# A four-layer graph network: all work between its edge stages laid out as pipelines over chunks of node blocks

## The reference, cut to what is computed

```python
# layer 0: attention (GATv2), 2 heads, with its own layer norm and relu ahead
h = relu(layernorm(x) * gamma + beta)
xl, xr = h @ Wl + bl, h @ Wr + br                      # [3125, 2*128]
alpha = softmax_by_dst((leaky_relu(xl[src] + xr[dst]) * att).sum(-1))
out = segment_sum(xl[src] * alpha, dst).mean(heads) + h @ res_W + bias + x
x = layernorm(x + out)
# layer 1: attention, 1 head, a scalar edge weight; gelu; batch norm over the nodes
m = leaky_relu((x @ Wl + bl)[src] + (x @ Wr + br)[dst] + edge_weight @ We)
h = gelu(x + segment_sum(alpha * xl[src], dst) + bias_out)
x = layernorm(x + (h - h.mean(0)) * rsqrt(h.var(0) + 1e-5) * bn_gamma + bn_beta)
# layer 2: three GINE layers
for l in range(3):
    agg = segment_sum(relu(y[src] + edge_attr @ W_lin[l] + b_lin[l]), dst)
    y = relu(batchnorm(relu((y + agg) @ W1[l] + b1[l]) @ W2[l] + b2[l]))
x = layernorm(x + y)
# layer 3: an MLP on every edge, its sum by target, an MLP on every node
e = relu(relu([x[src], x[dst], edge_attr] @ W1 + b1) @ W2 + b2) @ W3 + b3
node = relu([x, segment_sum(e, dst)] @ Wn1 + bn1) @ Wn2 + bn2
x = layernorm(x + layernorm(x + node) * gamma + beta)
```

## Time and profile before

| what | value |
|---|---|
| median of three runs | 4907.62 us |
| the profiled execution | 4908.47 us, span 4906.63, mean granted TensorE clock 0.802 |
| PE busy | 4209.5 us, 86% |
| PE's weight loads (PEld) | 3195.1, 65% |
| DVE | 2583.4, 53% |
| ACT | 1656.7, 34% |
| POOL | 2588.5, 53% |

### The profile page before, as it was taken

One profiled execution on the slowest core, in us unless ns is written; L12 is line 12 of the kernel. 1 busy time (PEld: TensorE's weight loads), 2 busy tenths in 40 slices (PEclk: granted clock), 3 DMA queues, 4 the chain that ended last, 5 costly groups with the idle time before them and its releaser, 6 DMA issues. The chain is left out here.

```text
span 4906.6 us, 91167 instructions
## 1 busy us (share of the span) xinstructions
PE 4209.5 (86%) x20501; PEld 3195.1 (65%) x20715; DVE 2583.4 (53%) x5638; ACT 1656.7 (34%) x3154; POOL 2588.5 (53%) x2647
## 2 busy tenths in 40 slices
PE   2799999947777649998799959999489999999994
PEld 1577777734444448886688848888356666666663
DVE  4788888866666544443344423444454555455544
ACT  1466666635555421112111121111233333333332
POOL 0455555437777537774577727777043434343420
PEclk9899999979999955555555555555799999999997
DMA  2333333323333212221222212222032222222210
GB/s 66 86 100 99 99 101 98 83 51 77 77 78 77 55 46 68 68 68 42 67 69 68 68 40 68 68 68 68 19 88 73 74 73 74 73 74 73 74 51 13
DMA packets 249457, 341.32 MB, mean 70 GB/s; under 512 B 102167, under 2 KB 174692, under 8 KB 249150
## 3 DMA queue, kind: packets, MB, share of 16 engines
q0 software_dynamic: 101632, 237.91, 18.2%
q1 hardware_dynamic: 130206, 78.84, 6.6%
q10 hardware_dynamic: 17568, 24.01, 1.7%
HBM read 324.54 MB, written 15.96 MB: 69 GB/s over the span
## 5 line engine op out<-in xcount | busy, mean ns | idle before, releaser
L771 POOL DMA_INDIRECT gath<-source_rows_narrow,idx x1176 | 1140.5, 970 | 613.9 <-issue 335.6
L894 POOL DMA_INDIRECT gath<-source_rows,idx_all x488 | 492.5, 1009 | 811.6 <-PE psum L913 561.2
L789 PE MATMUL psum<-gine_lin,ea 32*128 32x128 f32 x2928 | 757.3, 436 | 63.9 <-DMA ea<-in_edge_attr 63.4
L799 PE MATMUL psum<-hot,pm 128*128 128x128 f32 x2928 | 759.7, 441 | 36.7 <-ACT pm L854 36.2
L789 PEld LDWEIGHTS psum<-gine_lin,ea 32*128 32x128 f32 x2928 | 650.4, 323 | 148.2 <-DMA ea<-in_edge_attr 85.8
L799 PEld LDWEIGHTS psum<-hot,pm 128*128 128x128 f32 x2928 | 652.0, 328 | 121.8 <-issue 70.5
L552 POOL DMA_INDIRECT gath<-source_rows,idx_all x488 | 463.2, 949 | 482.7 <-PE psum L599 224.1
L854 ACT ACTIVATE pm<-vs 128x512 f32<-128x512 f32 x366 | 230.4, 629 | 1333.4 <-DVE vs L824 1313.5
L552 POOL DMA_INDIRECT gath<-source_rows_narrow,idx_all x488 | 487.0, 998 | 235.8 <-issue 148.1
L824 DVE TENSOR_TENSOR vs<-psum,gath 128x512 f32<-128x512 f32 x366 | 253.2, 692 | 635.1 <-POOLq L766 446.7
L582 PE MATMUL psum<-lk,att_b 128*128 128x512 f32 x732 | 373.4, 616 | 93.9 <-DVE lk L672 93.2
(11 more groups left out here) (188 smaller groups left out, 5609.9 us busy)
## 6 DMA issues: line engine op xcount, KB each, us to landing
rel<-rel_rows SPq DMA_DIRECT2D x366, 128.0 KB
ea<-in_edge_attr ACTq DMA_DIRECT2D x366, 64.0 KB
gath<-source_rows_narrow,idx POOLq DMA_INDIRECT x1176
gath<-source_rows,idx_all POOLq DMA_INDIRECT x976
gath<-source_rows_narrow,idx_all POOLq DMA_INDIRECT x488
ea<-in_edge_attr SPq DMA_DIRECT2D x122, 64.0 KB
source_rows<-stage SPq DMA_DIRECT2D x12, 512.0 KB, 2.9
source_rows_narrow<-TMP SPq DMA_DIRECT2D x3, 1600.0 KB, 7.3
```

Of the source, the lines that this page charges most:

```text
L771: pool.indirect_dma_start(out=gath[:, slot, j, 0:D], out_offset=None, in_=table1, in_offset=bass.IndirectOffsetOnAxis(ap=idx[:, slot, j:j ...
L789: last = e.matmul(E[s][:, j * D:(j + 1) * D], ea[:, s, j * P:(j + 1) * P], gine_lin[:, :], start=True, stop=True)
L799: last = e.matmul(O[s], pm[:, s, j * P:(j + 1) * P], hot[:, s, j, :], start=(j == 0), stop=(j == SUBS - 1))
L894: pool.indirect_dma_start(out=gath[:, i % 4, j, :], out_offset=None, in_=table, in_offset=bass.IndirectOffsetOnAxis(ap=idx_all[:, i, j:j + ...
```

## The change

Each stretch between two edge stages becomes one pipeline, or two, over seven chunks of four node blocks (`CB` = 4; the last chunk has one block). Each engine's instructions are written chunk by chunk, with semaphores that count chunks, so that no barrier stands between a norm, a turn and a product.

- **Row stages** (`rows_to_tables`, four calls): per chunk DVE computes mean and variance by `bn_stats` and `bn_aggr`, ACT the root, DVE reciprocal and shift, ACT the normalized rows (one instruction a block), PE turns them, ACT copies them (with gamma, beta and relu in layer 0), PE multiplies by Wl, DVE adds the bias, SP stores the chunk. On DVE the scale of a chunk comes behind the statistics of the next, and the bias add three chunks behind.
- **Target rows** (`TargetRows`) are not made in the row stage any more but at the head of the next edge stage, ahead of the walk on PE, ACT and DVE, while POOL's first gathers run. For the attentions their bias is a second matmul into the same bank: a row of ones (one partition) by the bias row. The first attention's also makes `Y` = 2x + h @ res_W + bias there. DVE's `memset` of `ACC` and its first `hot_t` come behind.
- **Setup** is merged into the first row stage: the loads are spread over SP's and ACT's queues, x comes in seven pieces, GINE's weights are all loaded here, the cutting of indices and edge weights is POOL's work instead of DVE's. The nine `weight_rows` stores are issued by SP at the end of the first attention's items.
- **Second row stage**: the heads' mean is one DVE instruction per block and head, inside the chunk.
- **End of the second attention** (`third_rows`): 25 sums, per chunk turned, gelu (with bias_out inside), statistics of 512 columns by `bn_stats`; then the batch norm's scale, and a second pipeline that shifts, turns back, adds the residual and makes GINE's first table with its bias.
- **GINE** is a Python loop over three layers. `gine_nodes`: seven adds, an MLP in chunks of 512 columns with two banks each way, `bn_stats`, then normalize, turn, add the bias and store by chunks; the last layer adds the residual instead.
- **Tail** (`node_out`): one pipeline of eight lags for the node MLP, both layer norms and the output, in rounds.

The core of the diff, with the new functions' loops:

```diff
-setup()
...
-with nc.Fori(0, GINE_LAYERS) as layer:
-    gine_node_to_table(layer)
-    gine_edges(layer)
-    gine_mlp(layer)
-    batchnorm("gine_bn", XT[:, :], gine_cols[:, 2:3], gine_cols[:, 3:4], ACT.Relu, sems=bn_sems, layer=layer)
-    transposes(XT, Z, *back_sems, base=layer * (NODE_BLOCKS // CH))
...
-node_mlp()
-transposes(HT, flat(Y))
-layernorm(Y[:, :, :], Y[:, :, :], gamma=bias("L3_gnn_gamma"), beta=bias("L3_gnn_beta"), prep=add_residual, prep_steps=1)
-layernorm(Y[:, :, :], Y[:, :, :], prep=add_residual, prep_steps=1)
...
+            for c in range(CHUNKS):
+                sp.wait_ge(row_staged, first_unit[c] + units_of[c])
+                sp.dma_start(out_rows[:, c * CB:c * CB + BLOCKS_OF[c], :],
+                             stage[:, c * CB:c * CB + BLOCKS_OF[c], :]).then_inc(row_stored, 16)
...
+            def stats(c):
+                a, n = c * CB, BLOCKS_OF[c]
+                if chunk_in is not None:
+                    v.wait_ge(chunk_in[c], 16)
+                if chunk_prep is not None:
+                    chunk_prep(v, step, a, n)
+                for b in range(a, a + n):
+                    last = v.bn_stats(row_stats[:, b, :], rows[:, b, :])
+                step(last)
+                for b in range(a, a + n):
+                    last = v.bn_aggr(row_mv[:, b, :], row_stats[:, b, :])
+                last.then_inc(row_var, 1)
+            def scales(c):
+                a, n = c * CB, BLOCKS_OF[c]
+                v.wait_ge(row_sd, base + c + 1)
+                step(v.reciprocal(row_scale[:, a:a + n], row_scale[:, a:a + n]))
+                v.scalar_tensor_tensor(row_shift[:, a:a + n], row_mv[:, a:a + n, 0], -1.0, row_scale[:, a:a + n],
+                                       ALU.mult, ALU.mult).then_inc(row_counted, 1)
...
+                for k in range(units_of[c]):
+                    u, m = first_unit[c] + k, min(per, n - k * per)
+                    v.wait_ge(row_made, u - unmade + 1)
+                    v.tensor_tensor(stage[:, a + k * per:a + k * per + m, :],
+                                    bank(u)[:, 0:m * width].rearrange("p (b w) -> p b w", w=width),
+                                    b_src.unsqueeze(1).broadcast_to([P, m, width]), ALU.add).then_inc(row_staged, 1)
...
+            if dve_first is not None:
+                dve_first(v, step)
+            for c in range(CHUNKS):
+                stats(c)
+                if c >= 1:
+                    scales(c - 1)
+                if c == 3 and bias_in is not None:
+                    v.wait_ge(bias_in, 16)
+                if c >= 3:
+                    add_bias(c - 3)
+            scales(CHUNKS - 1)
+            add_bias(CHUNKS - 3)
+            if dve_last is not None:
+                dve_last(v, step)
+            add_bias(CHUNKS - 2)
+            add_bias(CHUNKS - 1)
...
+            if act_first is not None:
+                act_first(a)
+            for c in range(CHUNKS):
+                deviations(c)
+                if c >= 1:
+                    normalize(c - 1)
+                if c == 2 and cols_in is not None:
+                    a.wait_ge(cols_in, 16)
+                if c >= 2:
+                    copy_turned(c - 2)
+            normalize(CHUNKS - 1)
+            copy_turned(CHUNKS - 2)
...
+            for c in range(CHUNKS):
+                turn(c)
+                if c == 1 and weights_in is not None:
+                    e.wait_ge(weights_in, 16)
+                if c >= 1:
+                    products(c - 1)
+            products(CHUNKS - 1)
+            if pe_last is not None:
+                pe_last(e)
...
+    def tensor(self, e):
+        w = self.width
+        for u in range(self.units):
+            a, m = self.blocks(u)
+            if u >= 4:
+                e.wait_ge(xr_rest, self.base + u - 3)
+            for j in range(m):
+                o = psum[:, u % 4, j * w:(j + 1) * w]
+                last = e.matmul(o, XT[:, (a + j) * P:(a + j + 1) * P], self.w_dst, start=True, stop=self.b_dst is None)
+                if self.b_dst is not None:
+                    last = e.matmul(o, ones_row[:, :], self.b_dst[0:1, :], start=False, stop=True)
+            last.then_inc(xr_made, 1)
+        if self.extra is not None:
+            for c in range(CHUNKS):
+                if c >= 4:
+                    e.wait_ge(xr_extra_out, c - 3)
+                for k in range(BLOCKS_OF[c]):
+                    o = psum[:, 4 + c % 4, k * D:(k + 1) * D]
+                    e.matmul(o, XT[:, (c * CB + k) * P:(c * CB + k + 1) * P], self.extra[0], start=True, stop=False)
+                    last = e.matmul(o, ones_row[:, :], self.extra[1][0:1, :], start=False, stop=True)
+                last.then_inc(xr_extra, 1)
+            e.wait_ge(xr_extra_out, CHUNKS)
+        e.wait_ge(xr_rest, self.base + self.units)
+        e.wait_ge(xr_third, self.base + self.units)
...
+        for u in range(self.units):
+            v.wait_ge(xr_first, self.base + u + 1)
+            if u >= 2:
+                v.wait_ge(xr_third, self.base + u - 1)
+            v.tensor_tensor(self.rest(u), self.bank(u), self.part(u, 0), ALU.subtract).then_inc(xr_rest, 1)
+            if u >= 1:
+                v.wait_ge(xr_rest, self.base + u)
+                third(u - 1)
...
+        step(pool.tensor_copy(dst_f, dst_i))
+        step(pool.tensor_scalar(dst_f, dst_f, gb_f[:, 2:3], -1.0, ALU.subtract, ALU.max))
+        step(pool.tensor_scalar(dst_f, dst_f, float(P), None, ALU.min))
+        pool.tensor_copy(src_f, src_i)
+        step(pool.tensor_copy(rel_b, dst_f))
+        pool.dma_start(rel_rows, rel_b).then_inc(rel_stored, 16)
+        pool.wait_ge(loads, 8 * 16)
+        m = [0]
+        for x, parts in ((ew_i, weight_parts), (we_f, we_p)):
+            for k, part in enumerate(parts):
+                step(pool.tensor_copy(part, x), weight_split, m)
+                if k < SPLIT - 1:
+                    step(pool.tensor_tensor(x, x, part, ALU.subtract), weight_split, m)
...
+def gat_edges(number, heads, dram, att, with_weight, target):
...
+            if not with_weight:
+                sp.wait_ge(weight_split, 5)
+                for a in range(SPLIT):
+                    for b in range(SPLIT):
+                        sp.dma_start(weight_rows[:, SPLIT * a + b, :], weight_parts[a]).then_inc(weight_stored, 16)
...
+            target.tensor(e)
+            walk(e, front, back, mid, tail, number)
...
+    def mean_of_heads(v, step, a, n):
+        for h in range(2):
+            for b in range(a, a + n):
+                last = v.scalar_tensor_tensor(Y[:, b, :], acc[:, b, h, :], zsum[:, b, h:h + 1], Y[:, b, :], ALU.mult, ALU.add)
+            step(last)
...
+            for c in range(CHUNKS):
+                v.tensor_tensor(h[:, at(c)], h[:, at(c)], XT[:, at(c)], ALU.add).then_inc(gn_h, 1)
+            for c in range(CHUNKS):
+                v.wait_ge(gn_y, base + c + 1)
+                last = v.bn_stats(col_stats[:, c, :], XT[:, valid(c)])
+            last.then_inc(gn_stat, 1)
+            v.wait_ge(gn_stat, layer + 1)
+            bn_dve(v, gamma, beta)
+            for c in range(CHUNKS):
+                v.wait_ge(gn_turned, base + c + 1)
+                rows = bank_of(4 + c % 4, c).rearrange("p (b d) -> p b d", d=D)
+                a, n = c * CB, BLOCKS_OF[c]
+                if more:
+                    v.tensor_tensor(TMP[:, a:a + n, :], rows, gine_blin[:, layer + 1, :].unsqueeze(1).broadcast_to([P, n, D]),
+                                    ALU.add).then_inc(gn_rows, 1)
...
+            first(0)
+            for c in range(1, CHUNKS):
+                first(c)
+                second(c - 1)
+            second(CHUNKS - 1)
...
+            a.wait_ge(gn_h, base + CHUNKS)
+            hidden(0)
+            for c in range(1, CHUNKS):
+                hidden(c)
+                output(c - 1)
+            output(CHUNKS - 1)
...
+for layer in range(GINE_LAYERS):
+    gine_edges(layer)
+    gine_nodes(layer)
+rows_to_tables(Y, X, XT, HID, weight("L3_gnn_W1a"), bias("L3_gnn_b1"), table,
+               ACC[:, :].rearrange("p (b d) -> p b d", d=HID))
+mlp_edges(TargetRows(HID, weight("L3_gnn_W1b"), None))
...
+            def residual(c):
+                a, m = c * CB, BLOCKS_OF[c]
+                y = Y[:, a:a + m, :]
+                v.wait_ge(nd_normed, count(0, c))
+                step(v.tensor_tensor(y, y, gamma.unsqueeze(1).broadcast_to([P, m, D]), ALU.mult))
+                step(v.tensor_tensor(y, y, beta.unsqueeze(1).broadcast_to([P, m, D]), ALU.add))
+                step(v.tensor_tensor(y, y, X[:, a:a + m, :], ALU.add))
+                stats(c)
...
+            counted_blocks(0)
+            for k in rounds:
+                if chunk(k, -1):
+                    counted_blocks(k + 1)
+                if chunk(k, 3):
+                    added(k - 3)
+                if chunk(k, 5):
+                    residual(k - 5)
+                if chunk(k, 3):
+                    scales(k - 3, 0)
```

(2 more changed lines are left out.)

983 lines of the change are left out of this document (540 added, 443 removed).

## The result

The changed kernel takes 4692.41 us, the median of four runs (4683.83 to 4696.89), beside 4908.78 (4905.48 to 4915.18) for the kernel before: 0.9556 of it (95% interval 0.9538 to 0.9573). It is 216 us faster, not 298 as forecast, and the time lies 7 us above the top of the stated range. The profiled execution has a span of 4692.1 us. The experiments further down came in four series, each on one chip with the kernel before beside it (5634, 5711, 4912 and 4919 us, by which a series is named here); in the first two of them index loads and gathered rows landed later, so a time is compared only within its series, or as a ratio to the kernel before of the same series.

A forecast was written before the change was run, and what follows sets the result against it. Edge stages were bound by PE (first attention, MLP), POOL (second attention) or nearly both (GINE); seams, 706 us, left engines idle. Gains between stages less costs at heads summed to -297.5 us: 4908.5 to 4610, range 4585 to 4655, with rivals 4555 to 4685.

The forecast's parts named there:

- First attention's head: Target rows ahead of the walk on PE, 64 us at the low level; V 71 us after the first gather; +62 us.
- Second attention's head: 100 target-row instructions, 21.5 us at the low level; V at 24.5, 17th gather at 37; +15 us.
- First stretch: Start to the first gather: POOL's setup chain, taken as 15 us, frees the barrier at 42; 116 us less.
- Edge MLP's head: Target rows without bias products; DVE leads, then memset; V at 24 us against 8.7; +15 us.
- tail: After the edge MLP, 121.9 us before: DVE lags from the sixth round, 81 us expected; gain 41.
- third stretch: Between second attention and GINE's first edge stage, 89.1 us before: 43 expected; gain 46.
- GINE's seams: Two stretches between GINE's edge stages, 69.5 us each before: 31 each expected; gain 77 together.
- second stretch: Between first and second attention, 68.4 us before: 34 expected with DVE's chunks at 4.5 us; gain 34.
- (a): Rival: target-row stretches run at PE's high level, 29 us less at the first head, 9 at the second; 4572; chance 0.22.
- (b): Rival: chunks don't overlap in the row stages and tail, each waiting for the one ahead; 4735 us; chance 0.13.
- (c): Rival: the edge MLP stays at PE's 1.2 GHz behind the target rows; slower than before, 5800 us; chance 0.02.
- (d): Rival: the target rows at the heads don't count since gathers cover them; 4518 us; chance 0.05.

## Why the prediction was wrong, point by point

- **First attention's head, the step that failed.** "At the low level two instructions of N=256 take 0.85" was taken from the earlier trace rows, where both have operands of 128 rows. The level was right (granted clock 0.50 throughout) and so was its reason, the single row: the ones over 128 rows bring the upper level. The pace was not: the term of 64 us came to 93.7, at 0.575 an instruction of 256 columns and not 0.425. The mix paid 0.30 us a switch, so 0.15 an instruction, 200 of them, 29.7 us, a cost that the sum put at nothing. So neither of the signs that I had named (0.425 apart, 0.22 apart) was seen. The trace before had this too: GINE's mix of 32 and 128 rows takes 489.25 us for 1949 instructions of 128 columns, 0.25 each where the lower level alone would be 0.21. With 16 an item that is 0.6 us too much, again 0.30 for each of an item's two switches. I used that row for the clock and not for the pace. With V at 100.8 instead of 71, the stage was 97.3 longer, not 62; 29.8 of the 35 are this, and some 5 stand behind V, where it isn't shown what takes them.
- **Second attention's head.** The same mis-sized term: 100 instructions in 35.7 us instead of 21.5, V 41.4 after the first gather (1050.82) instead of 24.5, the 17th gather at 54.9 instead of 37. +28.1 instead of +15: 17.9 us by that gather, less 5.1 by which the 488 gathers happened to be shorter than in the kernel before (481.9 against 487.0 us).
- **First stretch.** The price of POOL's passes was right, 16.5 us for the chain against 15 taken. What came late was x: six pieces of 256 KB and one of 64 beside 1.8 MB of loads for later stages, GINE's weights among them, which the change put on a second queue. 8 of the 14 us are shown to be that; with the loads moved, the other 6 are POOL's chain, which there starts 4 us later than I had it and takes 1.5 more.
- **Edge MLP's head.** +23.8 against +15: V 3 us later, and a fall to the lower level in PE's waits ahead of the walk, 4 more until it rose; some 2 us aren't traced. It is the one head with 128-row operands alone, and it ran high.
- **Seams and tail.** Right within 4 us each: third stretch 46.1 against 46, GINE's seams 75.5 against 77, the last 74.2 against 75.5, tail 37.2 against 41, the second stretch 30.4 against 34. bn_stats took 0.87 for four and bn_aggr 0.38, as taken (0.20 and 0.10). In the tail PE ended 17 us before the end and not 30.
- **Rivals.** (a) is out: the target rows did not run high; the ones over 128 rows show what that gives, V at 42.2 for the 42 of (a). By the Trainium skill (TensorE: Matmul & The Clock Gate, part 1) PE's activity releases the clock; the 93.7 us of back-to-back instructions at 1.2 GHz speak against busy-ness alone; the run with 128 rows agrees with the page, as the level rose after 4.4 us. (b) is out: DVE is busy for 75% of the second stretch (28.37 of 38.04 us, under the 80% I had named and over (b)'s 50%) and its chunks follow with gaps under 1 us from 972 to 1000. (c) is out: the edge MLP was at 0.99. (d) is out: POOL waited 97.84 and 35.16 us for the two heads.
- **The Trainium skill on GpSimd** (GPSIMD Engine Reference, 3.1 Elementwise) has a two-input add 1.96 times slower than on VectorE. Here a two-input subtraction took 1.16 us for 122x512 against 0.69, 1.7 times, and the two-scalar passes 2.01 and 1.50 against some 0.45, over three times; a copy 0.61 against 0.43.
- **The range** was too narrow by that step: the heads' products had a lower and an upper level as bounds, both from rows of one kind of operand, and none for the mix. The forecast's own low end was also set at 4585, where its terms (-14 and -7) give 4589.

## What to carry to other kernels

A bias as a product of a one-row operand looks like the cheapest instruction there is, and was the dearest part of this change: it cost 0.30 us at each switch and kept the whole stretch at 1.2 GHz. Fill such an operand with zero rows up to 128, or let the engine that reads PSUM add the bias; these few changed lines gave 80 us more, beside the 216 of the whole rebuilding. The same remedy in the GINE stages made PE faster and the kernel not, since PE doesn't set them. And when work is moved to the head of another stage, take its pace from a row with the same mix of operands, not from one with the same columns.

## What the runs showed of the hardware that was not expected

- A switch of PE between a stationary operand of 1 row and one of 128 costs 0.30 us at the lower level (3.40 us of columns a bank: 4.00 with two switches, 4.60 with four), and some 0.19 at the upper (0.41 against 0.22 for two instructions of 128 columns).
- 93.7 us of back-to-back PE instructions with half of its columns over one row stayed at 1.2 GHz; the same columns over 128 rows rose after 4.4 us. At the second attention's head PE came in at 2.4 GHz, fell after 1.6 us of that mix, and stayed up with 128 rows. GINE's edge stages went from 0.50 to 0.75 when their 32-row operand was filled up.
- 488 gathers of the same rows took 956 to 1005 ns each in executions of like kernels on one chip, 24 us in a stage that POOL sets; a gain under 10 us can't be read from this kernel's total, only from the windows of its stage.
